# Attention and quantised layer in one software pipeline: banks for the last tiles, setup in parts, idle products, another order

## What is computed

```python
x = x + _layernorm(attention(_layernorm(x), ln_w, ln_b, w_q, w_kv, w_o, theta))
x = x + _layernorm(ffn(_layernorm(x), weight, bias))
```

## Time and profile before

| | before |
|---|---|
| median of 3 runs | 720.86 us (719.91 to 723.58) |
| profiled execution | 720.5 us |
| its span, first to last instruction | 718.6 us |
| TensorE, VectorE, ScalarE, GpSimd busy | 664.2, 590.5, 562.4, 370.4 us |
| mean granted TensorE clock | 0.966 of full speed |

### The profile page before, as it was taken

How to read it: one execution, slowest core, us unless ns; L and a number is a source line. 1 busy time by engine, 2 the same in 40 slices (tenths; PEclk the granted TensorE clock), 3 DMA queues, 4 the chain that set the end, 5 groups by cost and what they waited for, 6 DMA issues and landing times.

```text
span 718.6 us, 19340 instructions
## 1 busy us (share of the span) xinstructions
PE 664.2 (92%) x6276; PEld 496.4 (69%) x6276; DVE 590.5 (82%) x1443; ACT 562.4 (78%) x1546; POOL 370.4 (52%) x724
## 2 busy tenths in 40 slices
PE   2678999999999999999999999999999999998654
PEld 1545667777787777777777877777777777765443
DVE  5999878988888888889888898888898888855552
ACT  2437889889888988888898888888888989887432
POOL 3454445655556565565555565555656556432332
PEclk9969999999999999999999999999999999999865
DMA  5101010201102020202012020202020010102000
GB/s 163 31 1 60 1 61 1 68 16 33 59 2 82 9 82 9 81 10 74 18 31 60 3 81 10 82 10 82 9 70 22 3 60 2 52 8 60 23 15 31
DMA packets 28705, 28.30 MB, mean 39 GB/s; under 512 B 2368, under 2 KB 28480, under 8 KB 28608
## 3 DMA queue, kind: packets, MB, share of 16 engines
q1 hardware_dynamic: 27792, 26.27, 11.9%
q10 hardware_dynamic: 816, 0.79, 0.3%
HBM read 18.66 MB, written 8.39 MB: 38 GB/s over the span
## 4 chain that ended last, share of the span: by engine, by line
PE 82%; DVE 9%; issue 4%; ACT 2%; DMA 2%; POOL 1%; SPq 0%; POOLq 0%; DVEq 0%; ACTq 0%
PE ps_f L466 11%; PE ps_mt L589 9%; PE ps_o L513 8%; PE ps_o L516 7%; PE ps_w L416 4%; PE ps_w L419 4%; PE ps_w L417 4%; PE ps_o L537 4%; PE ps_qk L416 4%; PE ps_tr L487 4%; PE ps_qk L419 4%; PE ps_qk L417 4%; PE ps_tr L416 2%; PE ps_tr L419 2%; PE ps_tr L417 2%
## 5 line engine op out<-in xcount | busy, mean ns | idle before, releaser
L691 ACT ACTIVATE feat<-ps_f 128x512 f32<-128x512 f32 x256 | 154.5, 606 | 14.1 <-PE ps_f L466 13.7
L366 DVE TENSOR_TENSOR kf<-kf 128x768 f32<-128x768 f32 (+1 forms) x128 | 140.8, 1100 | 2.0
L466 PE MATMUL ps_f<-qT,selr 128*128 128x512 f32 x320 | 140.9, 449 | 0.4 <-ACT qT L768 0.4
L1213 POOL TENSOR_TENSOR ve_y<-var_y,epst 128x1 f32<-128x1 f32 x64 | 12.4, 194 | 183.7 <-ACT squares_y L794 183.7
L589 PEld LDWEIGHTS ps_mt<-kf,vp 128*32 128x32 f32 x2048 | 66.4, 112 | 43.2 <-issue 38.6
L589 PE MATMUL ps_mt<-kf,vp 128*32 128x161 f32 x2048 | 84.1, 306 | 2.8 <-ACT rm L720 1.4
L735 ACT ACTIVATE hT<-ps_tr,lnb,lnwx 128x128 f32<-128x128 f32 x128 | 51.6, 453 | 30.4 <-PE ps_tr L498 30.4
L466 PEld LDWEIGHTS ps_f<-qT,selr 128*128 128x128 f32 x320 | 59.9, 189 | 20.5 <-issue 15.8
L1195 POOL TENSOR_TENSOR hT_l<-hT,hT_h 128x256 fp32r<-128x256 f32 x64 | 48.6, 760 | 48.7 <-ACT hT_h L745 48.7
L513 PE MATMUL ps_o<-feat,main 128*32 128x512 f32 x512 | 67.8, 602 | 0.2 <-issue 0.2
L516 PE MATMUL ps_o<-feat,rm 128*32 128x512 f32 x512 | 66.7, 592 | 0.0
(11 more groups left out here) (170 smaller groups left out, 2016.8 us busy)
## 6 DMA issues: line engine op xcount, KB each, us to landing
xc<-L_attn_x SPq DMA_DIRECT2D x16, 512.0 KB, 4.4
result<-fin SPq DMA_DIRECT2D x64, 128.0 KB, 1.7
xa<-L_attn_x SPq DMA_DIRECT2D x15, 512.0 KB, 4.0
wkqv<-L_attn_w_kv ACTq DMA_DIRECT2D x2, 256.0 KB, 4.4
xa<-L_attn_x SPq DMA_DIRECT2D x1, 384.0 KB, 5.1
csel<-shape_constants SPq DMA_DIRECT2D x1, 320.0 KB, 5.4
wkqv<-L_attn_w_q ACTq DMA_DIRECT2D x1, 256.0 KB, 4.6
wf<-L_ffn_weight SPq DMA_DIRECT2D x1, 256.0 KB, 5.4
```

What stands on the lines that cost most here:

```text
L366: return eng.tensor_tensor(dims(row, F_MAIN, [[FW, heads], [HD, NR], [1, HD]]), dims(row, F_LIN, [[FW, heads], [0, NR], [1, HD]]), dims(ro ...
L466: pe.matmul(ps_f[i % 2][:, :], selr[:, i], qT[:, par, quad], start=True, stop=True).then_inc(sel_done, 1)
L691: act.activation(feat[:, p2, i], ps_f[i % 2][:, :], ACT.Square).then_inc(squared, 1)
```

## The change

The lags and the lists of all engines are written anew. `FIRST` and `FINAL` shift single tiles among the first 8 and the last 12 to other steps. For the last two sequences (tiles 56 to 63), `turn_quads` and `turn_attention` use ps_mt0 and ps_mt1 in turn, and `ffn` uses ps_qk; the stages that read them do the same. The weight's quantisation is cut into seven parts, and all setup parts have a lag and a place in the lists. TensorE issues idle products of the constant tile `one`: 12 at step 0, two at each of 16 places in the first steps (into ps_o, before any `attend`), and two at each of 20 places that come after the last `select_4` (into ps_f1). 20 of the 24 `drain` places fulfil that condition: 12 of drain_a and 8 of drain_b. The two reloads `xc` of the first sequences are issued at steps 2 and 6, where nothing makes them wait.

The diff, cut; of lists only the new one stands where the order is all that changes:

```diff
 LAG = {
+    "fill_a": 0, "select_1": 7, "warm_up": 0, "turn_ffn_input": 15, "turn_ffn_weight": 12, "drain_a": 16,
+    "rest_matrix": 4, "fill_b": 2, "attend": 8, "sum_features": 3, "project_v": 1, "select_2": 7,
+    "turn_attention": 12, "ffn": 15, "select_3": 7, "turn_q": 3, "turn_sums": 3, "select_4": 7, "project_kq": 1,
+    "turn_quads": 11, "turn_z": 0, "drain_b": 14, "select_0": 6, "project_out": 12,
...
+    "from_grid": 15, "frequencies": 1, "weight_sizes": 11, "cast_selection": 4, "low_kq": 1, "extend_k": 3,
+    "block_maxima": 14, "add_ffn": 16, "weight_result": 12, "invert_denominators": 12, "low_v": 1, "split_bias": 10,
+    "scales": 14, "normalise_attention": 12, "products_0": 3, "products_1": 3, "weight_scales": 7,
+    "low_ffn_weight": 13, "stats_x": 0, "weight_candidate_high": 8, "weight_candidate_low": 7, "centre_wo": 2,
+    "low_ffn_input": 15, "moments_x": 0, "inverse_scales": 14, "rope_cos": 2, "add_attention": 13, "rope_sin": 2,
+    "constant": 3, "to_grid": 14, "weight_choice": 11, "centre_ffn_weight": 12, "rope_add": 2, "angles": 1,
+    "weight_distances": 10, "normalise_x": 0, "low_attention": 12, "low_wo": 8,
...
+FIRST = {
+    "fill_a": (0, 1, 0, 2, 1, 1, 0, 0), "fill_b": (0, 0, -2, -2, -3, -3, -4, -2),
+    "turn_z": (-1, 0, 0, 0, 0, 0, 0, 0),
...
+    "add_x": (-1, 0, 0, 0, 0, 0, 0, 0), "rstd_x": (-1, 0, 0, 0, 0, 0, 0, 0),
+}
+
+FINAL = {
+    "turn_ffn_input": (0, 0, 0, 0, 0, 0, 0, 0, 0, 0, 0, 2), "drain_a": (4, 3, 4, 4, 0, 0, 6, 5, 0, 0, 2, 1),
+    "ffn": (0, 0, 0, 0, 0, 0, 0, 0, 0, 0, 1, 2), "drain_b": (0, 0, 0, 0, 6, 6, 5, 7, 6, 5, 4, 3),
+
+    "from_grid": (0, 0, 0, 0, 0, 0, 0, 0, 0, 0, 0, 2), "add_ffn": (0, 0, 0, 0, 0, 0, 0, 0, 0, 2, 3, 2),
+    "low_ffn_input": (0, 0, 0, 0, 0, 0, 0, 0, 0, 0, 1, 2), "to_grid": (0, 0, 0, 0, 0, 0, 0, 0, 0, 0, 0, 2),
+}
+EARLY, LATE = 8, 12
...
+        def out_bank(t):
+
+            return ps_mt[1 - t.n % 2] if t.n > TILES - NT * 2 else ps_o
+
+        def ffn_bank(t):
+
+            return ps_qk if t.n > TILES - NT * 2 else ps_w
...
+            def idle_products(to, count):
+
+                for _ in range(count):
+                    pe.matmul(to[:, 0:P], one[:], one[:], start=True, stop=True)
+
+            def warm_up():
+                idle_products(ps_o, 12)
+
+            def fill():
+
+                if issued["attend"] == 0:
+                    idle_products(ps_o, 2)
+
+            def drain():
+
+                if issued["select_4"] == TILES:
+                    pe.wait_ge(squared, CHUNKS * TILES)
+                    idle_products(ps_f[1], 2)
...
+            def out_bank_is_free(t):
+
+                if t.n > TILES - NT * 2:
+
+                    pe.wait_ge(rm_copied, NS)
+                    wait(pe, norm_ready, last_in_bank("turn_quads", t))
+                    wait(pe, aT_low, last_in_bank("turn_attention", t))
+                else:
+                    wait(pe, o_copied, issued["attend"])
+                    wait(pe, norm_ready, issued["turn_quads"])
+                    wait(pe, aT_low, issued["turn_attention"])
...
             def ffn(t):
...
                 pe.wait_ge(xdT_low, t.n)
-                wait(pe, xs_ready, tiles(t.m, t.k - 1, LAG["project_out"]))
-                wait(pe, fin_ready, tiles(t.m, t.k - 1, LAG["ffn"]))
+                if t.n > TILES - NT * 2:
+
+                    pe.wait_ge(qk_read, 2 * TILES)
+                    wait(pe, fin_ready, t.n - 1)
...
             def project_out(t):
...
-                wait(pe, fin_ready, tiles(t.m, t.k, LAG["ffn"]))
+                wait(pe, fin_ready, min(issued["ffn"], TILES - NT * 2))
...
+            def step(n):
+                early(n, "fill_a", fill)
+                each(n, "select_1", select, 1)
+                setup(n, "warm_up", warm_up)
+                each(n, "turn_ffn_input", turn_ffn_input)
+                setup(n, "turn_ffn_weight", turn_ffn_weight)
+                late(n, "drain_a", drain)
+                once(n, "rest_matrix", rest_matrix)
+                early(n, "fill_b", fill)
+                each(n, "attend", attend)
+                each(n, "sum_features", sum_features)
+                each(n, "project_v", project_v)
+                each(n, "select_2", select, 2)
+                each(n, "turn_attention", turn_attention)
+                each(n, "ffn", ffn)
+                each(n, "select_3", select, 3)
+                each(n, "turn_q", turn_q)
+                once(n, "turn_sums", turn_sums)
+                each(n, "select_4", select, 4)
+                each(n, "project_kq", project_kq)
+                each(n, "turn_quads", turn_quads)
+                each(n, "turn_z", turn_z)
+                late(n, "drain_b", drain)
+                each(n, "select_0", select, 0)
+                each(n, "project_out", project_out)
```

More of the change, by code:

```diff
@@ L64 @@
 LAG = {
[L65 to L76, removed]
@@ new lines, with stage_steps @@
+FINAL = {
[5 more added lines that the diff above has]
+EARLY, LATE = 8, 12
+def stage_steps(count):
+    plan = {}
+    for stage, lag in LAG.items():
+        steps = plan.setdefault(stage, {})
+        for tile in range(count):
+            step = tile + lag
+            if tile < EARLY:
+                step += FIRST.get(stage, (0,) * EARLY)[tile]
+            elif tile >= count - LATE:
+                step += FINAL.get(stage, (0,) * LATE)[tile - count + LATE]
+            steps.setdefault(step, []).append(tile)
+    return plan
@@ L147, in sandwich, with __init__, each, once @@
     TILES = NS * NT
[L148 to L157, removed]
-    class Tile:
[L162 to L179, removed]
+    plan = stage_steps(TILES)
+    issued = {stage: 0 for stage in plan}
+    class Tile:
+        def __init__(self, index):
+            self.n = index + 1
+            self.tile, self.seq = index % NT, index // NT
+            self.par, self.load = self.seq % 2, self.seq // 2 + 1
+            self.two, self.four = index % 2, index % 4
+    def each(n, name, stage, *args):
+        for index in plan[name].get(n, ()):
+            stage(Tile(index), *args)
+            issued[name] += 1
+    def once(n, name, stage):
+        for index in plan[name].get(n, ()):
+            if index % NT == NT - 1:
+                stage(Tile(index))
+    def setup(n, name, stage):
+        if n == LAG[name]:
+            stage()
+    def early(n, name, stage):
+        for index in plan[name].get(n, ()):
+            if index < EARLY:
+                stage()
+    def late(n, name, stage):
+        for index in plan[name].get(n, ()):
+            if index >= TILES - LATE:
+                stage()
     def wait(eng, sem, count):
@@ L184, in wait, with every_step @@
             eng.wait_ge(sem, count)
[L186 to L192, removed]
+    def every_step(step):
+        used = {n for steps in plan.values() for n in steps}
+        for n in range(min(used), max(used) + 1):
+            step(n)
     with ExitStack() as ctx:
@@ L470, in turn_ffn_input @@
                 pe.wait_ge(xd_ready, t.n)
-                wait(pe, hT_copied, tiles(t.m, t.k, LAG["turn_z"]))
-                wait(pe, qT_copied, tiles(t.m, t.k, LAG["turn_q"]))
-                wait(pe, xdT_low, tiles(t.m, t.k - 1, LAG["turn_ffn_input"]))
-                wait(pe, v_copied, tiles(t.m, t.k, LAG["project_v"]))
+                wait(pe, hT_copied, issued["turn_z"])
+                wait(pe, qT_copied, issued["turn_q"])
+                wait(pe, xdT_low, issued["turn_ffn_input"])
+                wait(pe, v_copied, issued["project_v"])
                 for c in range(CH):
```

406 lines of the change are left out of this document (207 added, 199 removed).

## The result

The changed kernel takes 691.69 us (691.14 to 692.01), against 722.22 (719.91 to 723.59) for the kernel before on the same chip (the three runs of the table above and a fourth): a ratio of 0.958, 95% interval 0.9548 to 0.9611. The profiled execution has a span of 690.0 us, 28.6 less than before. A second build of the same kernel, run later beside the last experiments, gave 691.88, again 0.958.

A forecast was written before the change was run, and what follows sets the result against it. TensorE was taken to bound the middle, VectorE the fill, a chain of waits the end. 720.5 - 5.5 (fill) - 4 - 6 - 5.5 (drain) - 0.5 (store waits) + 0.4 gave 699.4 us, range 690 to 711.

The forecast's parts named there:

- Steady order: Middle tiles: TensorE has no idle time there, so the new order was to gain 0 us.
- Rival 1: Steady tiles: VectorE holds sum_features, slack 0.28 us; 0.54 us lost per tile, 725.9 us; chance 0.06, or 0.09 below 0.44 us.
- Start: Start to turn of z of tile 2: setup ahead of angles lets z come earlier, 3 us gained, bounds 0 and 4.
- the clock term: Last tile: idle products holding 2.4 GHz speed up 21 products; 1 us taken, 2.7 if held, 0 if not.
- Tiles 2 to 7: Fill: four weight quantisation parts leave the stretch where VectorE bounds; 10 us gained, bounds 6 and 12.
- Tiles 7 to 14: Later fill: the moved 13.9 us return and VectorE bounds the stretch; 7.5 us lost, bounds +0.7 and -13.9.
- Drain, tiles 56 to 60: Alternating ps_mt banks and ps_qk for ffn remove waits for attT_l and fin; 4 us gained, bounds 0 and 5.
- rival 3: Drain: in-order queues, not banks, bind it; half of 15.5 us gained, 707 us; chance 0.15.
- Tiles 60 to 63: Separate banks cut three steps of 7.0 us to about 5.0 each; 6 us gained, bounds 0 and 9.4.
- Last tile: From tile 63's turn to the end: fewer waits behind other tiles, and a faster clock; 5.5 us gained, bounds 0 and 10.
- Store waits: Drain: two waits on stores no longer met because the drain is looser; 0.5 us gained.
- Rivals 2 and 4: 2: moved setup not absorbed, fill gives 0, 705 us, chance 0.13. 4: idle products do nothing in the drain, 700 to 702.

## Why the prediction was right, and where it was off

The direction, the cause and both places hold; 691.69 lies in the range, near its low end, 7.7 us under the forecast and 1.3 under the 693 to 706 that I had given to both gains coming about as summed. In the spans, 7.1 us are missing: I had some gains 12.2 us too small in all and others 5.1 too large. Of the signs I had named, tile 7 came at 54.3 (near 53), tile 14 at 114.1 (near 119), the weight operations from 46.7 to 87.2 (55 to 105), the last turns of quads 4.0 apart (5) and the end 18.4 after them (20).

Some of the prediction's sums don't close: 63.6 + 2.5 is 66.1 and not 65.8; the bounds of the fill's terms add up to -7.9 and 16.7, not to -1 and 12; the upper bound of 5 for tiles 56 to 60 lies over the 3.9 that its own floor of 24.3 allows; and the upper bounds of fill and last tile give 688.4, not 690.

**Steady order, 0: right.** 485.4 us for 49 tiles, 9.91 each. Rival 1 failed, and its slack was 0.55 us, not 0.28.

**Start, 3 us: right in kind, 4.3 measured**, 0.3 over my upper bound. VectorE begins z of tile 1 at 14.95, 0.45 before the forecast's 15.4, and TensorE turns it at 15.41; tile 2 then follows after 4.8 us and not 6. The size is uncertain by more than a microsecond: in the kernels whose start is the changed kernel's, tile 2 is turned between 19.4 and 21.7. The start also holds more than the new order: k's and q's weights are now waited for apart from v's, and the two reloads of x stand earlier. No run undoes these one by one. The trace shows the clock as the prediction's durations did. TensorE in the changed kernel, and then without any idle products:

```profile
11.47 0.28 PE L484 MATMUL ps_tr<-wkqv_l,hT_h 128*128 128x256 f32 x1
```

```profile
11.40 0.42 PE L484 MATMUL ps_tr<-wkqv_l,hT_h 128*128 128x256 f32 x1
...
18.30 0.27 PE L484 MATMUL ps_tr<-wkqv_l,hT_h 128*128 128x256 f32 x1
```

The products come at 2.4 GHz 7 us earlier. It moves nothing there: tile 2 is turned at 20.21 with them and 20.27 without, as tile 1's z waits for VectorE (15.41 and 15.22). The Trainium skill (TensorE: Matmul & The Clock Gate, "What's actually happening") has activity release the throttled state, and the trace agrees with it. The upper end of the clock term, 2.7 us for the last tile, is too high for this kernel: without the idle products the last tile lost 1.1 us in one trace and 0.7 in another. On the kernel before, with the clock at 0.57 there, they gave 3.0; the denser work of the new banks had taken most of that already.

**Tiles 2 to 7, 10 us: 7.9.** The four parts left. Of the new ones, `weight_scales` and `weight_candidate_low` of step 7 run before tile 7, between 46.66 and 50.61, but they are not what is missing: one step later, tile 7 is turned at 54.37 all the same. The five steps took 6.9, 6.0, 6.2, 6.9 and 8.1 us. In the last one TensorE is idle for 0.8 us only, 0.7 of it before `sum_features`, waiting for ScalarE's copy of the rest matrix; with every variant of the weight parts this step takes 8.1. My sum had VectorE's work and the loop of z in it, but not what TensorE itself does in these steps with its shorter lags. Which of its stages makes the difference stays open.

**Tiles 7 to 14, -7.5 us: the step that failed; -1.5 measured.** I took VectorE's sum, 49.7 + 13.9 = 63.6 us, over TensorE's 57.6, and added 2.5 for stretching and a wait. Neither came: TensorE waits 0.8 us in all here, and for no weight part. VectorE was busy 54.81 us, and TensorE's 58.31 bounded the stretch. Of the 8.8 us between the sum and 54.81, 3.4 are the seven operations that ran before tile 7, and 0.6 are the gaps in the 13.9 (13.29 busy). Most of the rest is that the operations did not stretch: they shrank. In the changed kernel:

```profile
49.92 0.69 DVE L1028 SCALAR_TENSOR_TENSOR wb<-wq 128x512 f32<-128x512 f32 x1
...
74.22 0.68 DVE L1036 TENSOR_TENSOR wq<-wq,wa 128x512 f32<-128x512 f32 x1
74.94 0.69 DVE L1037 TENSOR_TENSOR wq<-wq,wb 128x512 f32<-128x512 f32 x1
75.66 0.69 DVE L1038 TENSOR_TENSOR wb<-wb,wa 128x512 f32<-128x512 f32 x1
...
78.47 1.71 POOL L414 TENSOR_TENSOR kf<-kf 128x256 f32<-128x256 f32 x1 [4.63 <-DVE kf L1144]
```

The same operation that took 1.10 us at 42.36 takes 0.69 at 75.66. In its new place it runs in the 4.63 us in which GpSimd waits for VectorE's kf, and not beside hT_l and low_q. The 19 operations took 13.4 us before and 11.9 now (the last, `wf`, is still long, 1.04 at 86.19, with GpSimd at work from 85.64); between tiles 7 and 14 z (553 to 408 ns a piece, 1.0 us for seven), kf's copy (348 to 220, 0.9 us) and one operation of the bias (878 to 354) are shorter too. My argument, that later steps hold more GpSimd work and so more stretching, used the amount of work and not whether it stands beside. Nor is it enough to stand beside: in the kernel before, VectorE's operation at 41.63 takes 0.69 with GpSimd's beside it all along, and there it is GpSimd's that is long:

```profile
32.25 0.73 POOL L1195 TENSOR_TENSOR hT_l<-hT,hT_h 128x256 fp32r<-128x256 f32 x1 [2.27 <-ACT hT_h L745]
...
41.65 1.26 POOL L1195 TENSOR_TENSOR hT_l<-hT,hT_h 128x256 fp32r<-128x256 f32 x1 [2.27 <-ACT hT_h L745]
```

The hT_l at 32.25 begins before VectorE's operation of 1.10 us (32.43), the one at 41.65 just behind VectorE's of 0.69. In these rows it is the later one of the two that is long. That the two engines stretch each other is argued from such rows; no kernel isolates it. The bound that I had for "all hidden", 57.6, was the nearer one.

**Drain, tiles 56 to 60, 4 us: 1.1 (28.2 to 27.1).** The wait of turn_quads for attT_l did go, and undoing the out bank lengthens these four tiles to 29.4 us, so the bank is worth 2.3 here. But with both old banks the new order takes 29.4 too, 1.2 more than the kernel before: that part of the change loses, and I had not counted it. ScalarE's squares were late next, as I wrote, but at 6.8 us a tile and not at the floor of 6.1. TensorE is idle for 4.5 of the 27.1 us: three waits of the last selections for `feat`, 3.1 us, and the wait for `fin` of 1.5. ScalarE is itself idle for 6.9; the two wait for each other over ps_f. So rival 3 holds in part for these four tiles.

**Tiles 60 to 63, 6 us: 8.9; 4.0 us a tile instead of 5.0.** The mechanism is the one named, and undoing it shows its size: 19.1 us with the ffn bank undone, 18.1 with both, for 12.2. My 5.0 added a serial chain turn, xdT_l, ffn, quads, project_out; the stages of different tiles overlap more than that. What sets 4.03 us now is a ring through ffn. In the changed kernel, TensorE, ScalarE, GpSimd, VectorE and TensorE again:

```profile
670.71 0.37 PE L657 MATMUL ps_qk<-bias,ones 128*128 128x256 f32 x1
...
671.82 0.38 ACT L912 ACTIVATE squares_f<-ps_qk 128x256 f32<-128x256 f32 x1
...
672.64 0.55 POOL L1333 TENSOR_TENSOR rs_f<-ve_f,mhalf 128x1 f32<-128x1 f32 x1
...
673.22 0.48 DVE L1228 SCALAR_TENSOR_TENSOR fin<-ps_qk,rs_f,xs 128x256 f32<-128x256 f32 x1 [0.67 <-POOL rs_f L1333]
...
673.90 0.42 DVE L1170 TENSOR_TENSOR att<-ps_mt,rden 128x256 f32<-128x256 f32 x1
...
674.58 0.41 PE L606 MATMUL ps_mt<-small,att 128*128 128x128 f32 x2 [0.97 <-DVE att L1170]
674.74 0.37 PE L657 MATMUL ps_qk<-bias,ones 128*128 128x256 f32 x1
```

`rden` and `att` of the last tile are behind `fin` on VectorE, which waits 0.67 us for the root, and the next ffn is behind the turn of that attention. By these rows it is an order, not a bank; another place of `fin` was not tried.

**Last tile, 5.5 us: 7.1.** I gave the banks 0.8 of the 8.3 us of waits and the FINAL shifts the rest. The runs show the reverse: undoing the ffn bank lengthens this stretch from 18.4 to 24.8 us, undoing both to 27.1, undoing the shifts to 18.8. The waits "behind other tiles' work" were there, it seems, because those tiles were held by the bank themselves.

**Store waits, 0.5 us:** the two waits of `fin` for a store, 2.5 us together in the kernel before, are gone.

**Rivals 2 and 4** failed: the fill gave 10.7 us, and the clock was 1.00 in the drain, up to tile 63 by the denser work alone.

## What to carry to other kernels

Before a pipeline drains, list the PSUM banks of stages that have ended and give one to the stage whose result is read latest (here ffn, read by `fin` after a root); 14 of 29.9 us came from that. Move setup of the critical engine to the point at which another engine becomes the bound, and try a step on either side: the first parts one step on cost 2.5 us, all of them four to five steps earlier 7.4. Idle products are for a drain that cannot be made dense; look at the granted clock after the waits are gone.

## What the runs showed of the hardware

- VectorE's two-input operations of 128 x 512 f32 took 0.67 to 0.69 us where GpSimd waited, and 1.07 to 1.10 where they began while one of GpSimd's was running. One that began first (41.63 in the kernel before) kept its 0.69, and GpSimd's hT_l beside it took 1.26 and not 0.73.
- An idle 128 x 128 product of f32 operands shows as two matmul records. After the clock has risen, 20 records take 2.39 us, 0.12 each; the 28 of the start, 4.69 us, 0.17 each.
- TensorE's granted clock stayed at 1.00 through tiles 60 to 63 without idle products once the waits on the banks were gone, where it had been 0.68 with them; it fell to 0.77 in the last tile. With idle products but both old banks it was 0.91 over the drain.
